# A perceiver block on one core: another order of work between its two attentions

## The reference

```python
x = x + LN(softmax(q(LN(x)) k(ctx)^T / 8) v(ctx) @ Wo + bo + LN(x)) * gamma + beta   # cross attention, 16 heads of 64, 512 keys per batch
x = x + attention(LN(x))                                                           # 16 heads of 32, rotary, 64 keys
x = x + mixture_of_experts(LN(x))                                                  # 8 experts, the best 2 of each token
```

## Time and profile before

| | |
|---|---|
| median of 3 runs | 1828.1 us (1827.56 to 1829.45) |
| profiled execution, its own time | 1827.18 us |
| span of its instructions | 1825.4 us |
| PE / DVE / ACT / POOL busy | 93% / 47% / 37% / 16% of the span |
| mean granted TensorE clock | 0.963 of full speed |

### The profile page before, as it was taken

The page is one execution under the profiler, slowest core; times in us unless marked ns, Lnnn a source line. Parts: engine busy times, 40 slices in busy tenths (PEclk is TensorE's granted clock), DMA queues, the critical chain, the costliest instruction groups (busy, mean ns, idle before and its releaser), DMA issues. The chain is left out here.

```text
span 1825.4 us, 27192 instructions
## 1 busy us (share of the span) xinstructions
PE 1701.0 (93%) x10906; PEld 1427.8 (78%) x10906; DVE 850.8 (47%) x1590; ACT 676.0 (37%) x1304; POOL 293.3 (16%) x249
## 2 busy tenths in 40 slices
PE   7999999999999999999999679874999989989996
PEld 6888888888888888888887557663888878879885
DVE  4343434434334344343433866554656447446731
ACT  5333333333333333333333334333545335334521
POOL 4210111101111011110100213445110011110101
PEclk9999999999999999999999889885999999999998
DMA  6500811001110111101024501114746345446611
GB/s 232 199 27 30 142 53 50 25 35 50 53 50 20 40 50 53 50 18 42 4 76 149 176 24 40 40 35 134 243 142 206 114 127 193 132 114 188 214 33 20
DMA packets 54091, 165.37 MB, mean 91 GB/s; under 512 B 10580, under 2 KB 10964, under 8 KB 53376
## 3 DMA queue, kind: packets, MB, share of 16 engines
q1 hardware_dynamic: 38032, 131.88, 21.2%
q0 software_dynamic: 15888, 31.19, 7.5%
HBM read 143.54 MB, written 55.64 MB: 109 GB/s over the span
## 5 line engine op out<-in xcount | busy, mean ns | idle before, releaser
L406 PE MATMUL psum<-ctx,Wk 128*128 128x512 f32 x1536 | 385.0, 399 | 0.0
L406 PE MATMUL psum<-Wv,ctx 128*128 128x512 f32 x1536 | 368.7, 389 | 0.0
L406 PEld LDWEIGHTS psum<-Wv,ctx 128*128 128x128 f32 x1536 | 288.3, 188 | 59.9
L406 PEld LDWEIGHTS psum<-ctx,Wk 128*128 128x128 f32 x1536 | 279.2, 188 | 55.5
L406 PE MATMUL psum<-xgT,Wh 128*128 128x256 f32 (+2 forms) x1536 | 273.8, 330 | 23.0 <-issue 23.0
L406 PEld LDWEIGHTS psum<-xgT,Wh 128*128 128x128 f32 x1536 | 243.3, 195 | 45.3 <-issue 25.6
L870 DVE SCALAR_TENSOR_TENSOR kT<-psum,bkc,kT 128x512 fp32r<-128x512 f32 x128 | 96.0, 750 | 387.9 <-ACT kT L1237 387.9
L747 PE MATMUL psum<-Wh,hs 128*128 128x512 f32 x1056 | 260.5, 392 | 0.1
L747 PEld LDWEIGHTS psum<-Wh,hs 128*128 128x128 f32 x1056 | 194.2, 188 | 37.0 <-DVE hs L1126 0.2
L1237 ACT ACTIVATE kT<-psum,bkc 128x512 fp32r<-128x512 f32 x128 | 88.3, 690 | 247.5 <-PE psum L406 247.4
L1403 ACT ACTIVATE gl<-psum,b1c 128x256 f32<-128x256 f32 (+2 forms) x128 | 71.1, 555 | 270.9 <-PE psum L406 269.3
(11 more groups left out here) (146 smaller groups left out, 1766.6 us busy)
## 6 DMA issues: line engine op xcount, KB each, us to landing
raw<-in_W SPq DMA_DIRECT2D x128, 512.0 KB, 3.7
expert_rows<-in_spare_rows SPq DMA_DIRECT2D x16, 1042.0 KB, 7.9
raw<-in_ctxT SPq DMA_DIRECT2D x32, 512.0 KB, 4.0
xg<-expert_rows POOLq DMA_DIRECT2D x32, 256.0 KB, 3.7
low_parts<-Olo POOLq DMA_DIRECT2D x32, 128.0 KB, 2.3
oT<-low_parts SPq DMA_DIRECT2D x8, 512.0 KB, 5.1
out_x<-x SPq DMA_DIRECT2D x12, 256.0 KB
xs<-in_x SPq DMA_DIRECT2D x4, 512.0 KB, 6.7
```

The lines of the kernel that those rows point to most:

```text
L406: mm = pe.matmul(dst, l, r, start=n == 0, stop=n == len(pairs) - 1)
```

## The change

- TensorE: `turn(n - 2)` is issued ahead of `c_product` in the last steps of the cross attention.
- VectorE: sum and statistics of tile t stand first in round t; `o_low` of the last weighing moves from ahead of the rounds to the end of round 1, and the shift of tile 0 to round 1; the eight `split_lo` of WA leave VectorE.
- ScalarE: `nx_normal(t - 2)` stands ahead of `split_high(WA t)`; the high part of the last weighing (`o_high(31)`) stands at the end of round 1, behind two WA splits; the first of these waits until all scores are made.
- GpSimd: it gets the eight `split_lo` of WA, each behind `x1_done` of its tile and ahead of that tile's second power; `low_store(31)` stands behind the first two powers.
- SP's queue: two residuals and `gab` go ahead of `x1`, before the last weighing; the small loads go behind WA2 and WA3 and between the later ones; there are three `ya` buffers; `ya`, `gab`, `nxc` and `wrp` lie at other addresses.

```diff
+                if 0 <= n - 2 < NS:
+                    turn(n - 2)
                 if NS - 1 <= n <= NS + 1:
                     c_product(n - NS + 1)
-                if 0 <= n - 2 < NS:
-                    turn(n - 2)
...
-            o_low(NS // HALF - 1)
...
             for t in range(NT + 2):
-                if 0 <= t - 2 < NT:
+                if t < NT:
+                    v.wait_ge(ya_in[t % 3], 16 * (t // 3 + 1))
+                    v.wait_ge(c_psum, t + 1)
+                    v.tensor_tensor(ya[t % 3][:], c_bank(t), ya[t % 3][:], ALU.add).then_inc(c_sum, 1)
+                    row_stats(ya[t % 3][:], t % 2, ya_stat, t, (c_sum, t + 1))
+                if 1 <= t - 2 < NT:
                     shift(2 + t % 2, x1_pow, t - 2, x1_shift)
                 if 0 <= t - 1 < NT:
                     c_scale(t - 1)
+                if t == 1:
+                    shift(2, x1_pow, 0, x1_shift)
                 if 0 <= t - 2 < NT:
                     nxT_low(t - 2)
...
-                    split_lo(L_WA + t, Wa[w][1][:, 2 * c:2 * c + 2, :], Wa[w][0][:, 2 * c:2 * c + 2, :])
+                if t == 1:
+                    o_low(NS // HALF - 1)
...
             for t in range(NT + 2):
+                if 0 <= t - 2 < NT:
+                    nx_normal(t - 2)
                 if t < NT:
                     w, c = divmod(t, 2)
+                    if t == 0:
+                        s.wait_ge(s_psum, NS)
                     split_high(L_WA + t, Wa[w][0][:, 2 * c:2 * c + 2, :])
-                if 0 <= t - 2 < NT:
-                    nx_normal(t - 2)
+                if t == 1:
+                    o_high(NS // HALF - 1)
...
-            low_store(2 * B - 1)
-
+            power(rstd2[:, 0, 0:1], ya_pow, ya_stat, 3)
             for t in range(NT + 2):
+                if t == 1:
+                    power(rstd2[:, 2, 0:1], x1_pow, x1_stat, 3)
+                    low_store(2 * B - 1)
                 if 0 <= t - 1 < NT:
+                    w, c = divmod(t - 1, 2)
+                    g.wait_ge(x1_done, t)
+                    split_lo(L_WA + t - 1, Wa[w][1][:, 2 * c:2 * c + 2, :], Wa[w][0][:, 2 * c:2 * c + 2, :])
+                if 1 <= t - 1 < NT:
                     power(rstd2[:, 2 + (t - 1) % 2, 0:1], x1_pow, x1_stat, 3 * (t - 1) + 3)
-                if t < NT:
-                    power(rstd2[:, t % 2, 0:1], ya_pow, ya_stat, 3 * t + 3)
+                if t + 1 < NT:
+                    power(rstd2[:, (t + 1) % 2, 0:1], ya_pow, ya_stat, 3 * t + 6)
```

SP's queue from the last weighing on, after the change:

```diff
+            residual(0)
+            residual(1)
+            sp.dma_start(gab[:], a["gamma"].partition_broadcast(P)).then_inc(c_vectors_in, 16)
             for h in range(4):
                 sp.dma_start(x1[:, 2 * h:2 * h + 2, :], ...)
             fetch_attention(0)
             fetch_attention(1)
             low_part(4)
             low_part(5)
             sp.wait_ge(o_psum, NS)
+            residual(2)
+            low_part(6)
+            residual(3)
+            low_part(7)
+            for v in range(4):
+                sp.wait_ge(low_out[v], 16 * NT)
+            fetch_attention(2)
+            fetch_attention(3)
...
```

More of the change, by code:

```diff
@@ L79, in perceiver_block @@
         ones = small("ones", [P, P], BF16)
+        wrp = small("wrp", [P, KD, E])
         maskb = small("maskb", [P, NT, E], BF16)
         maskc = small("maskc", [P, NT, E], BF16)
-        c0 = 3.625
+        c0 = 3.75
         QO = place("QO", c0, [P, NJ, T])
@@ L111, in perceiver_block @@
         x1 = place("x1", c0 + 32, [P, NT, D])
-        gab = place("gab", o + 82, [P, D])
-        ya = [place(f"ya{r}", o + 90 + 2 * r, [P, D]) for r in range(2)]
-        nxc = place("nxc", o + 94, [P, D])
+        gab = place("gab", o + 88, [P, D])
+        ya = [place(f"ya{r}", kb, [P, D]) for r, kb in enumerate((o + 90, c0 + 60, o + 92))]
+        nxc = place("nxc", c0 + 62, [P, D])
         nxall = place("nxall", c0, [P, 2 * KD, T], F32R)
@@ L214, in perceiver_block @@
         c_vectors_in = sem("c_vectors_in")
-        ya_in = [sem(f"ya_in{r}") for r in range(2)]
+        ya_in = [sem(f"ya_in{r}") for r in range(3)]
         x1_in = [sem(f"x1_in{h}") for h in range(4)]
@@ L325, in sync_program @@
             sp.wait_ge(k_psum, NS)
+            sp.wait_ge(v_done, NS)
             sp.wait_ge(residual_added, 32)
-            for h in range(4):
-                sp.dma_start(x1[:, 2 * h:2 * h + 2, :], residuals[1, 2 * h * P:(2 * h + 2) * P].rearrange("(t p) d -> p t d", p=P)
-                             ).then_inc(x1_in[h], 16)
             def fetch_attention(t):
@@ L336, in residual @@
             def residual(t):
-                if t >= 2:
-                    sp.wait_ge(x1_done, t - 1)
-                sp.dma_start(ya[t % 2][:], residuals[0, t * P:(t + 1) * P]).then_inc(ya_in[t % 2], 16)
+                if t >= 3:
+                    sp.wait_ge(x1_done, t - 2)
+                sp.dma_start(ya[t % 3][:], residuals[0, t * P:(t + 1) * P]).then_inc(ya_in[t % 3], 16)
+            residual(0)
+            residual(1)
+            sp.dma_start(gab[:], a["gamma"].partition_broadcast(P)).then_inc(c_vectors_in, 16)
+            for h in range(4):
+                sp.dma_start(x1[:, 2 * h:2 * h + 2, :], residuals[1, 2 * h * P:(2 * h + 2) * P].rearrange("(t p) d -> p t d", p=P)
+                             ).then_inc(x1_in[h], 16)
             fetch_attention(0)
@@ L345, in sync_program @@
             sp.wait_ge(o_psum, NS)
[L346 to L367, removed]
@@ new lines, in sync_program @@
+            residual(2)
[6 more added lines that the diff above has]
+            fetch_attention(3)
+            for v in range(4):
+                sp.dma_start(absb[v][:], a[("abq", "abk", "abv", "abo")[v]].partition_broadcast(P)).then_inc(d_vectors_in, 16)
+            residual(4)
+            sp.dma_start(cosb[:], a["cos"]).then_inc(d_vectors_in, 16)
@@ new lines, in sync_program @@
+            sp.dma_start(sinb[:], a["sin"]).then_inc(d_vectors_in, 16)
+            fetch_attention(4)
+            sp.dma_start(brb[:], a["br"].partition_broadcast(P)).then_inc(r_in, 16)
+            sp.dma_start(wrp[:], a["Wr"].rearrange("(k p) e -> p k e", p=P)).then_inc(r_in, 16)
+            residual(5)
+            for dst, name in ((before, "before"), (ones, "ones"), (slot_from, "slot_from"), (row_of, "row_of")):
+                sp.dma_start(dst[:], a[name]).then_inc(e_in, 16)
+            fetch_attention(5)
@@ L369, in sync_program @@
+            for t in (6, 7):
+                residual(t)
+                fetch_attention(t)
             for i in range(3):
@@ L910, in c_scale @@
                     v.wait_ge(c_vectors_in, 16)
-                v.scalar_tensor_tensor(ya[r][:], ya[r][:], mv2[:, r, 0:1], gab[:], ALU.subtract, ALU.mult).then_inc(c_norm, 1)
+                v.scalar_tensor_tensor(y, y, mv2[:, r, 0:1], gab[:], ALU.subtract, ALU.mult).then_inc(c_norm, 1)
                 v.wait_ge(c_norm, t + 1)
                 v.wait_ge(x1_in[t // 2], 16)
-                v.scalar_tensor_tensor(x1[:, t, :], ya[r][:], rstd2[:, r, 0:1], x1[:, t, :], ALU.mult, ALU.add).then_inc(x1_done, 1)
+                v.scalar_tensor_tensor(x1[:, t, :], y, rstd2[:, r, 0:1], x1[:, t, :], ALU.mult, ALU.add).then_inc(x1_done, 1)
                 if t >= 2:
@@ L1219, in build_qbd, with o_high @@
                     s.activation(qbd[b % 2][0][rows, :, cols], QO[rows, :, b * TB:(b + 1) * TB], ACT.Copy).then_inc(qbd_hi, 1)
+            def o_high(u):
+                b, half = divmod(u, 2)
+                s.wait_ge(o_psum, HALF * (u + 1))
+                s.activation(Ohi[:, HALF * half:HALF * (half + 1), b * TB:(b + 1) * TB], bank[7][:, 0:HALF * TB].rearrange("p (s q) -> p s q", s=HALF),
+                             ACT.Copy).then_inc(o_hi, 1)
             s.wait_ge(q_done, 2 * NJ)
@@ L1245, in scalar_program @@
                     build_qbd(b + 1)
[L1246 to L1251, removed]
+                if n >= 6 and n % HALF == 2 and n < NS + 2:
+                    o_high(n // HALF - 1)
                 if 0 <= n - 2 < NS:
```

11 lines of the change are left out of this document (2 added, 9 removed).

## The result

The changed kernel took 1814.64 us (median of 5 runs, 1813.35 to 1816.68) against 1828.1 (median of 5, 1827.56 to 1834.48): a ratio of 0.9917, 95% interval [0.9906, 0.9929], 13.5 us by the medians. The forecast was 1812.4, within 1808.5 to 1818. The profiled execution took 1814.46 us for a span of 1812.7, again 1.8 us more.

What follows compares the result with a forecast made beforehand. TensorE's standing, chiefly waiting for nxc between the attentions, and then VectorE's round were taken as the bound. Span 1825.4 less 15.7 gives 1809.7; 1.8 around it gives 1811.5; 0.9 for the median gives 1812.4, range 1808.5 to 1818.

Steps and rivals of the forecast that it cites:

- Turns ahead: End of cross attention: TensorE's turns run ahead of the products, so the last weighing starts 1.3 us earlier.
- The early tiles and the wait of 10.96 us: Tiles 0 and 1 are prepared before the last result, so TensorE's 10.96 us wait before c_normal(0) goes entirely.
- The reading of the last link: Before c_normal(0): ScalarE stands 12.49 us before a WA split whose load is late, with the normalisation behind it.
- The one late load: WA2 lands at 1007.3, so TensorE stands 1.1 us before c_normal(1); 0.0 to 2.2 with other landing times.
- The small loads that "now cost nothing that I can find": SP's queue: the small loads, moved from ahead of everything to between later WA loads, were priced at no cost.
- The rounds at TensorE's pace: Rounds to c_normal(4): VectorE's round falls from 6.65 to 5.15 us, so TensorE's 6.06 us sets the pace.
- The tail: From c_normal(4) at 1027.3 to c_normal(7) at 1042.3, with two GpSimd splits, 4.8 us, on the path.
- Splits at 2.39: GpSimd's WA splits take 2.39 us each, since VectorE's work meanwhile has at most one SBUF tile.
- the first rival: GpSimd becomes the pace, splits up to 3.37 us: gains of only 10.5 to 13.5 us, 1814.6 to 1817.6; chance 0.17.
- the forecast's own: Whole kernel: the forecast's main case, gains of 13.5 to 17 us, 1811 to 1814.6; chance 0.60.
- The sum: c_normal(7) at 1042.3 instead of 1057.98, 15.7 us earlier, taking the span from 1825.4 to 1809.7.
- "Shifts as a block": Projections, second attention and experts behind c_normal(7) read the same tiles in the same order and keep the whole 15.7 us.

Runs made afterwards that it cites:

- turns_only: Kernel before with only TensorE's turn issued ahead of c_product; ratio 0.9987 to the kernel before.
- three_mended: Changed kernel with WA6 and WA7 low parts behind GpSimd's last power, residual 4 ahead of absb, tile 1's normalisation ahead of the WA2 split; ratio 0.9894.
- all_mended: three_mended with the deferred splits waiting for the last shift, and WA4, residual 5 and WA5 ahead of most small loads; ratio 0.9876.
- defer_behind_shift: Changed kernel with GpSimd's low parts of WA6 and WA7 moved behind its last power and begun only after the last shift; ratio 0.9904.
- result_first: Changed kernel with the last weighing's high part, low part and store again ahead of all sums; ratio 0.9938.
- small_first: Changed kernel with the small loads on SP's queue put ahead of low_part(6), about where they stood before; ratio 0.9932.
- split_first: Changed kernel with ScalarE's old order, split of WA t ahead of the normalisation of tile t - 2; ratio 0.9940.
- before_again: Kernel before, unchanged, run once more for a second trace; profiled only, stage 82.48 us.
- power_first: Changed kernel with GpSimd's second power of a tile ahead of the WA split instead of behind it; ratio 0.9923.

## Why the prediction was right, point by point

- *Turns ahead.* 1.16 us for 1.3; turns_only has it alone.
- *The early tiles and the wait of 10.96 us.* It went entirely, as forecast: `c_normal(0)` comes 25.75 us after `c_product(0)` instead of 38.05. Its causes, each put back by itself, cost 7.4 us (ScalarE's order), 5.2 us (small loads ahead of WA2) and 3.9 us (last result first, 2.1 of it a held shift). They aren't parts of a sum: each alone leaves TensorE standing at `c_normal(0)` or `(1)`, and each pays for the clock on top (2.5, 1.9 and 1.4 us), as the kernel before did. In the time of the whole kernel the three are 3 to 5 us each (0.9940, 0.9932 and 0.9938 beside 0.9917 and 0.9914), with intervals that touch those of the changed kernel, so their order of size is shown in the stage alone. The third `ya` buffer, the new addresses and the early residuals were not put back by themselves. The reading of the last link (ScalarE before a late load) was the right one.
- *The one late load.* TensorE stood 1.16 us before `c_normal(1)`, 1.1 in the forecast.
- *The small loads that "now cost nothing that I can find".* This step failed, and was small. Residual 4 stands behind the four `absb`; VectorE waited 2.12 us for it and TensorE 0.79 before `c_normal(2)`, 2.1 us in the second trace. three_mended and all_mended show it.
- *The rounds at TensorE's pace.* 1022.88 to 1028.81 is 5.93 us, 6.06 in the forecast. From `c_normal(0)` to `(4)` the forecast had 25.3 us and the trace has 26.1; the 0.8 is the wait before `c_normal(2)`, for residual 4.
- *The tail.* From `c_normal(4)` to `(7)` 1042.68 - 1028.81 = 13.9 us for 15.0. The power of tile 7 ended at 1033.6, while the products still ran, so the 0.4 us that I added for it wasn't there, and the handovers were shorter. That the two splits lie on the path there is shown by defer_behind_shift: without them 11.6 us (1041.04 - 1029.43). But that is 2.3 us less and not 4.8: with the splits gone, `c_normal(6)` comes without a wait, and the rest of the path holds.
- *Splits at 2.39.* All at 2.35 to 2.42. This and not the time rules out the first rival: 1814.64 lies just where its range (1814.6 to 1817.6) meets the forecast's own (1811 to 1814.6), but no split and no round is long. The reason given, that VectorE has nothing with two SBUF tiles meanwhile, was right for this order; the shift, which also has two, is free of them only because it waits for the power behind the split.
- *The sum.* 15.7 forecast; 16.0 in the stage over two traces each. The first pair of traces has 12.3 us of it at `c_normal(0)`, 0.4 in the rounds to `c_normal(4)` (26.51 to 26.09) and 3.3 in the tail (17.15 to 13.87); the forecast had 12.3, 1.2 and 2.2. So the mechanism was right, and that the two last misses, 0.8 too much and 1.1 too little, nearly cancel is luck.
- *"Shifts as a block".* This step isn't borne out. In the first pair of traces 15.3 us at `c_normal(7)` became 12.7 at the end, so the span was 1812.7 for 1809.7. The medians say 13.5, since the median lay 0.2 over the profiled execution and not 0.9. The sign that I had set for this, tiles of the second attention that change their length, did come: 211.9 us before, 207.8 and 215.4 after. One kernel alone shows as much, so the runs don't tell whether 3 us were lost to the change or to the execution.

The ratio's ends, 0.9906 and 0.9929, are 17.2 and 13.0 us below 1828.1, so 15.7 and 16.0 lie in it, and 13.5 too. A single pair of profiles can't tell 13 from 16.

## What to carry to other kernels

Where an engine waits, ask which instruction of the last link stands in front of the one that is wanted. Here that was a weight split before a late load, and reordering one engine was worth more in the stage than starting the data 12.5 us earlier. Price a long wait of TensorE with what comes behind it, too: after waits of 5 to 11 us its next 5.93 us of work took 7.3 to 8.4. Count a transfer's bytes against those queued before it, not only its issue. When work moves to GpSimd, list every VectorE instruction with two SBUF operands, the one-column ones too, and start the long GpSimd operation where none of them can fall due.

## What the runs showed of the hardware that was not expected

- A VectorE instruction on 128x1 elements with two SBUF operands took 2.29 to 2.31 us in place of 0.15 or 0.16 when a GpSimd subtraction of 128x1024 had begun 0.07 us before it.
- The kernel before took 1790 us on one chip and 1828 to 1839 on others. In the traces that I compared, the second attention alone differs by 41 us, 170.4 against 211.9 us, with the same instructions: TensorE stood there 20.8 us for "issue" on the slower chip and not at all on the other, at a mean granted clock of 0.80 against 0.87. The cause is open.
- TensorE's granted clock was lower after its long waits. The wait before `c_normal(0)` or `(1)` and the mean clock of the work behind it, 5.93 us long when undisturbed: 5.16 us and 0.80 (result_first), 5.98 and 0.75 (small_first), 7.58 and 0.69 (split_first), 10.96 and 0.81 (before), 11.17 and 0.76 (before_again), 11.22 and 0.69 (turns_only). After waits of up to 2.1 us in the rounds it was 1.00 in every kernel but power_first (1.96 us and 0.77). A longer wait did not mean a lower clock.
